# Fused cross-attention and expert layer: gate rows loaded before the zero stores, two tiles gated by VectorE alone, one rounding moved ahead

## The reference, cut to what matters

```python
...
A = jnp.maximum(jnp.abs(masked.sum(axis=0)), 1.0)
O = jnp.einsum('hst,bthe->bshe', A, V).reshape(b, s, dim)
mu = O.mean(axis=-1, keepdims=True)
var = O.var(axis=-1, keepdims=True)
Y = (O - mu) / jnp.sqrt(var + GN_EPS) * gn_gamma + gn_beta
W = jax.nn.relu(x @ wg_w)
return W * Y @ wo_w
...
x = x + attention(layernorm(x), ctx_2048, ctx_2048, ...)
x = x + experts(layernorm(x), ...)
```

## Time and profile before

| quantity | value |
|---|---|
| median of 3 runs | 965.88 us (965.65 to 966.13) |
| span of the profiled execution | 967.2 us |
| PE busy (matmul) | 936.7 us, 97% |
| DVE busy | 518.7 us, 54% |
| POOL busy | 484.5 us, 50% |
| ACT busy | 333.0 us, 34% |

### The profile page before, as it was taken

One profiled execution on the slowest core, in us unless ns is written; L12 is line 12 of the kernel. 1 busy time (PEld: TensorE's weight loads), 2 busy tenths in 40 slices (PEclk: granted clock), 3 DMA queues, 4 the chain that ended last, 5 costly groups with the idle time before them and its releaser, 6 DMA issues.

```text
span 967.2 us, 18994 instructions
## 1 busy us (share of the span) xinstructions
PE 936.7 (97%) x5222; PEld 832.9 (86%) x5223; DVE 518.7 (54%) x1026; ACT 333.0 (34%) x711; POOL 484.5 (50%) x345
## 2 busy tenths in 40 slices
PE   8999998899999989999999999999999999999998
PEld 5767886687889979999999999999999999989886
DVE  5546777888885543333333333333333333349886
ACT  4455554353324222333332333332233333232221
POOL 1116777773176674235535553555555505137760
PEclk9999999999999999999999999999999999999999
DMA  6739994665577667354435555434555422389972
GB/s 210 245 129 392 392 391 156 225 197 152 184 251 260 239 221 249 115 176 161 168 97 179 179 179 175 159 97 170 179 179 179 174 82 77 98 221 266 271 209 85
DMA packets 120646, 187.85 MB, mean 194 GB/s; under 512 B 13600, under 2 KB 71072, under 8 KB 117920
## 3 DMA queue, kind: packets, MB, share of 16 engines
q1 hardware_dynamic: 106704, 107.96, 34.4%
q0 software_dynamic: 13904, 79.44, 24.0%
HBM read 111.85 MB, written 75.50 MB: 194 GB/s over the span
## 4 chain that ended last, share of the span: by engine, by line
PE 78%; DVE 11%; issue 5%; ACT 3%; DMA 2%; POOL 1%; ACTq 0%; DVEq 0%; SPq 0%
PE ps L1050 14%; PE ps L1052 14%; PE ps L1051 14%; PE ps L1102 8%; PE ps L1104 7%; PE ps L1103 7%; PE ps L873 4%; DVE res L1600 2%; PE ps L914 1%; PE ps L923 1%; DVE st L1320 1%; DVE res L1318 1%; DMA gate_d<-gate_out 1%; PE ps L942 1%; PE ps L944 1%
## 5 line engine op out<-in xcount | busy, mean ns | idle before, releaser
L1050 PE MATMUL ps<-whi,xhi 128*128 (+1 forms) x896 | 299.7, 335 | 1.7 <-issue 1.2
L1052 PE MATMUL ps<-whi,xlo 128*128 (+1 forms) x896 | 290.0, 324 | 0.0
L1051 PE MATMUL ps<-wlo,xhi 128*128 (+1 forms) x896 | 289.6, 323 | 0.0
L1050 PEld LDWEIGHTS ps<-whi,xhi 128*128 128x128 f32 x896 | 169.4, 189 | 2.8 <-issue 2.1
L1051 PEld LDWEIGHTS ps<-wlo,xhi 128*128 128x128 f32 x896 | 170.3, 190 | 0.0
L1052 PEld LDWEIGHTS ps<-whi,xlo 128*128 128x128 f32 x896 | 169.2, 189 | 0.0
L783 ACT ACTIVATE sg<-ps 128x352 f32<-128x352 f32 x112 | 52.0, 464 | 299.0 <-PE ps L1052 299.0
L1369 DVE TENSOR_TENSOR hlo<-ps,hhi 128x384 fp32r<-128x384 f32 x112 | 62.3, 556 | 168.3 <-ACT hhi L826 168.2
L1347 DVE TENSOR_TENSOR hx<-ps,sg 128x352 f32<-128x352 f32 x112 | 58.6, 523 | 174.0 <-ACT sg L783 174.0
L527 POOL CAST whi<-raw 128x2816 fp32r<-128x2816 f32 x16 | 40.5, 2534 | 212.2 <-PE ps L1052 212.2
L1102 PE MATMUL ps<-whi,hhi 128*128 (+1 forms) x333 | 132.6, 398 | 4.1 <-DVE hlo L1369 4.1
(11 more groups left out here) (187 smaller groups left out, 1408.9 us busy)
## 6 DMA issues: line engine op xcount, KB each, us to landing
raw<-wexp_in POOLq DMA_DIRECT2D x18, 2176.0 KB, 9.5
xslot_d<-zero SPq DMA_DIRECT2D x10, 2048.0 KB, 21.6
xg<-xslot_d SPq DMA_DIRECT2D x320, 64.0 KB, 2.0
yslot_d<-ysb SPq DMA_DIRECT2D x80, 256.0 KB, 2.1
xg<-xn_d SPq DMA_DIRECT2D x128, 64.0 KB, 3.2
xq<-x_in SPq DMA_DIRECT2D x16, 256.0 KB, 3.5
gate_d<-gate_out SPq DMA_DIRECT2D x16, 256.0 KB, 2.6
yslot_d<-zero SPq DMA_DIRECT2D x2, 2048.0 KB, 18.5
```

The source lines that it names most:

```text
L1050: pe.matmul(ps[:, 2 + m, 0:INTER], xh, wh, start=(k == 0), stop=False)
L1051: pe.matmul(ps[:, 2 + m, 0:INTER], xh, wl, start=False, stop=False)
L1052: mm = pe.matmul(ps[:, 2 + m, 0:INTER], xl, wh, start=False, stop=(k == KT - 1))
```

## The change

Five edits. SP waits for the gate stores and loads gate rows and x rows of tiles 0 and 1 before the zero stores; the pipeline skips them later. `first_gates` on POOL prepares two tiles (four instructions instead of two, over all of head 2's context). On DVE tile 1 gets the same two instructions as tile 0, placed before the second block's statistics; `norm_o(1)`, `affine(1)` and `gate_o(1)` go, and `a_low(0)` moves ahead of `products(last, 2)`. The `wo_remainder` calls of the last two heads move behind the issue of the first expert's load. In the last head ACT rounds strip 0 before it takes the absolute value of strip 1.

```diff
@@ -254,7 +254,7 @@
         scat = sb3("scat", [P, XR, D], F32)
 
         wo_sb = raw[:, 1, 0:KT * D].rearrange("p (k n) -> p k n", k=KT)
-        gate_gamma, gate_beta = head_in[:, 0, 2 * S:3 * S], head_in[:, 0, 3 * S:4 * S]
+        gate_gamma, gate_beta = ([head_in[:, 0, (2 * t + i) * S:(2 * t + i + 1) * S] for t in range(2)] for i in range(2))
         gath = raw[:, :, :].rearrange("p a n -> p (a n)")[:, 0:GR * TOPK * D].rearrange("p (r k n) -> p r k n", r=GR, k=TOPK)
         ps = psum("ps", [P, 8, 512], F32)
 
@@ -354,6 +354,12 @@
             sp.dma_start(gn_sb[:, :, :], gn[None, :, :].to_broadcast([P, 2, D])).then_inc(w3_loaded, 16)
             sp.dma_start(wr_sb[:, :, :], wr.rearrange("(k p) n -> p k n", p=P)).then_inc(w3_loaded, 16)
 
+            for p in range(2):
+                sp.wait_ge(gate_stored[p], 16 * (NT // 2))
+            for t in range(2):
+                sp.dma_start(gin[:, t, :], rows(gate_d, t * ST)).then_inc(gate_loaded[t], 16)
+                sp.dma_start(xin[:, t, :], rows(x, t * ST)).then_inc(x3_loaded[t], 16)
+
             sp.wait_ge(zero_ready, 1)
             for c in range(NR // 8):
                 sp.dma_start(xslot_d[c * 8 * P:(c + 1) * 8 * P, :].rearrange("(p r) n -> p r n", p=P),
@@ -362,18 +368,16 @@
                 sp.dma_start(yslot_d[c * 8 * P:(c + 1) * 8 * P, :].rearrange("(p r) n -> p r n", p=P),
                              zero[:, None, :].to_broadcast([P, 8, D])).then_inc(y_zeroed, 16)
 
-
-            for p in range(2):
-                sp.wait_ge(gate_stored[p], 16 * (NT // 2))
-
             def load_gate(t, r, turn):
-                if type(t) is not int or t >= 2:
-                    sp.wait_ge(gated, t - 1)
+                if type(t) is int and t < 2:
+                    return
+                sp.wait_ge(gated, t - 1)
                 sp.dma_start(gin[:, r % 2, :], rows(gate_d, r * ST + turn)).then_inc(gate_loaded[r % 2], 16)
 
             def load_x3(t, r, turn):
-                if type(t) is not int or t >= 2:
-                    sp.wait_ge(x1_ready, t - 1)
+                if type(t) is int and t < 2:
+                    return
+                sp.wait_ge(x1_ready, t - 1)
                 sp.dma_start(xin[:, r % 2, :], rows(x, r * ST + turn)).then_inc(x3_loaded[r % 2], 16)
 
             def store_xn(t, r, turn):
@@ -486,13 +490,14 @@
                     pool.tensor_tensor(q_lo[:, b, :], q_sb[:, b, :], q_hi[:, b, :].bitcast(F32), ALU.subtract).then_inc(q_rest, 1)
 
             def first_gates():
-                pool.wait_ge(gate_loaded[0], 16)
                 pool.wait_ge(w3_loaded, 48)
                 pool.wait_ge(s_mm, ST * (H - 1))
-                pool.tensor_tensor(gate_gamma, gin[:, 0, :], gn_sb[:, 0, :], ALU.mult).then_inc(gate_affine, 1)
-                pool.tensor_tensor(gate_beta, gin[:, 0, :], gn_sb[:, 1, :], ALU.mult).then_inc(gate_affine, 1)
-                pool.sem_inc(o_gamma, 1)
-                pool.sem_inc(o_beta, 1)
+                for t in range(2):
+                    pool.wait_ge(gate_loaded[t], 16)
+                    pool.tensor_tensor(gate_gamma[t], gin[:, t, :], gn_sb[:, 0, :], ALU.mult).then_inc(gate_affine, 1)
+                    pool.tensor_tensor(gate_beta[t], gin[:, t, :], gn_sb[:, 1, :], ALU.mult).then_inc(gate_affine, 1)
+                pool.sem_inc(o_gamma, 2)
+                pool.sem_inc(o_beta, 2)
 
             def wo_remainder(h):
                 pool.wait_ge(wo_high, h + 1)
@@ -513,9 +518,12 @@
                 if h + 1 < H:
                     q_remainder(h + 1)
                     ctx_remainder(h + 1)
-                wo_remainder(h)
+                if h < H - 2:
+                    wo_remainder(h)
             pool.wait_ge(s_mm, ST * H)
             pool.dma_start(raw[:, 0, :], wexp[0, :, :]).then_inc(raw_loaded[0], 16)
+            for h in range(H - 2, H):
+                wo_remainder(h)
 
             def split(o, p, half, before):
 
@@ -552,7 +560,7 @@
                     pool.wait_ge(first_lo, t + 1)
                     pool.sem_inc(w13_ready, 1)
 
-            for t in range(1, NT):
+            for t in range(2, NT):
                 if t == B:
                     pool.wait_ge(wo_low, KT)
                     pool.wait_ge(o_mm, ST * H)
@@ -690,13 +698,15 @@
                 for j in range(ST):
                     act.wait_ge(s_mm, ST * h + j + 1)
                     n = S - P * j
+                    if j == 1 and h == H - 1:
+                        at_rounded(h, 0)
                     act.activation(at_sb[:, AT_OFF[j]:AT_OFF[j] + n], ps[:, 4 + j % 2, 0:n], ACT.Abs,
                                    scale=const[:, bass.ds(C_KDEC + h * ST + j, 1)]).then_inc(s_abs, 1)
                     if j == 1:
                         act.wait_ge(sum_mm, h + 1)
                         act.wait_ge(o_ready, ST * h)
                         act.activation(v_sum, ps[:, 6, :], ACT.Copy).then_inc(sum_ready, 1)
-                    if j:
+                    if j and (j > 1 or h < H - 1):
                         at_rounded(h, j - 1)
                 at_rounded(h, ST - 1)
                 if h + 1 < H:
@@ -755,8 +765,7 @@
                 act.activation(xT[:, p, :, :], ps[:, p, :], ACT.Copy).then_inc(a_xT, 1)
 
             std_o(0)
-            act.sem_inc(o_normed, 1)
-            norm_o(1)
+            act.sem_inc(o_normed, 2)
             evac_a(0, 0, 0)
             std_o(1)
             norm_o(2)
@@ -1239,15 +1248,15 @@
                     dve.wait_ge(v_ready, ST * h + tt + 1)
                     dve.tensor_tensor(v_lo[:, tt, :], ps[:, V_BANK[tt], :], v_hi[:, tt, :].bitcast(F32), ALU.subtract).then_inc(v_rest, 1)
 
-            def first_centred():
-                dve.wait_ge(gate_affine, 2)
-                dve.wait_ge(o_aggr, 1)
-                dve.scalar_tensor_tensor(gin[:, 0, :], o_sb[:, 0, :], mv3[:, 0, 0:1], gate_gamma, ALU.subtract, ALU.mult).then_inc(o_gated, 1)
-
-            def first_scaled():
+            def centred(t):
+                dve.wait_ge(gate_affine, 2 * t + 2)
+                dve.wait_ge(o_aggr, t + 1)
+                dve.scalar_tensor_tensor(gin[:, t, :], o_sb[:, t, :], mv3[:, t, 0:1], gate_gamma[t], ALU.subtract, ALU.mult).then_inc(o_gated, 1)
+
+            def scaled(t):
                 dve.wait_ge(o_rstd, 1)
-                dve.wait_ge(o_gated, 1)
-                dve.scalar_tensor_tensor(o_sb[:, 0, :], gin[:, 0, :], sd3[:, 1, 0:1], gate_beta, ALU.mult, ALU.add).then_inc(gated, 1)
+                dve.wait_ge(o_gated, t + 1)
+                dve.scalar_tensor_tensor(o_sb[:, t, :], gin[:, t, :], sd3[:, 1, t:t + 1], gate_beta[t], ALU.mult, ALU.add).then_inc(gated, 1)
 
             def a_low(t, r, turn):
                 p, half = r % 2, 2 * turn + r // 2
@@ -1279,15 +1288,16 @@
             last = H - 1
             products(last, 0)
             statistics(last, 0)
-            first_centred()
+            centred(0)
             products(last, 1)
             rstd_o(0)
-            first_scaled()
+            scaled(0)
+            centred(1)
+            scaled(1)
             statistics(last, 1)
+            a_low(0, 0, 0)
             products(last, 2)
             rstd_o(1)
-            gate_o(1, 1, 0)
-            a_low(0, 0, 0)
             products(last, 3)
             a_low(1, 1, 0)
```

## The result

| | before | after |
|---|---|---|
| median of 20 runs | 966.33 us | 969.19 us |
| ratio to before | | 1.0026, 95% interval 1.0017 to 1.0036 |
| span of the profiled execution | 967.2 us | 967.7 us |

The change made the kernel slower by 0.26%, about 2.5 us (interval 1.6 to 3.5). I had forecast 965.7 us, a gain of 0.2 us, with a range of 963.8 to 967.5. Put on the same 965.88 us, the measured ratio gives 968.4.

What follows compares the result with a forecast made beforehand. PE, busy 97% of the span, was taken to bound the kernel; only its waiting stretch could gain. The terms came to -0.22 us at tile 2: profiled 967.2 becomes 967.0, or 965.7 off the 965.88 median, range 963.8 to 967.5.

Steps and rivals of the forecast that it cites:

- The collision of the centring: DVE's centring of tile 0 collides with POOL's first moved remainder of wo and ends at 159.61, 0.26 us later than before.
- the three collisions of the trace before: DVE's centring of tile 0 and gates of tiles 1 and 2, each ending 0.54 to 0.55 us after a POOL instruction.
- POOL's end plus 0.55: Collision rule: a DVE instruction with all operands in SBUF, meeting a POOL instruction, ends 0.55 us after POOL's end.
- The rounding of strip 0: Last head: rounding fits ACT's idle 2.25 us before 151.77, removing POOL's 0.33 us wait; gain 0.33 us.
- The way from tile 0 to the gate of tile 2: Projection stage: statistics to norm 1.76 us, norm to POOL's add 3.68, gate collides, ending at 169.88 against 170.10.
- The late statistics: DVE's statistics of block 1, behind both scalings, start at 162.60 instead of 160.94, 1.66 us later, eating POOL's freed 2.7 us.
- Loads ahead of the zeros, four products: POOL's four gate products start without the 1.54 us DMA wait, ending at 150.2 against 150.5; later zero stores cost 0.
- The pattern of long tiles: Rival: POOL's lag keeps every projection tile long, 4.91 us instead of alternating with 4.09; +3.3 us, 968.9; chance 0.12.
- The escape of tile 2's gate: Rival: DVE's gate of tile 2 gets ahead of POOL's next product, ending at 168.75; gain 1.35, 964.5; chance 0.22.
- Half the worse pattern: Half of the +3.3 us from some 4 short projection tiles becoming long: 967.5, the slow end of the range.
- does not do what it says: Rival: tile 2's gate rows still arrive last, or ACT's new order loses the 0.33 us; 965.9 to 966.4; chance 0.16.
- Were DVE first: Alternative at the centring of tile 0: the remainders slide back and hit its scaling, ending about 161.6; bound +0.7 us.

Runs made afterwards that it cites:

- e1: Changed kernel, but POOL's two remainders of wo wait until tiles 0 and 1 are gated; ratio to before 0.9990 (0.9976 to 1.0003).
- e2: Changed kernel, but the second remainder of wo waits until the first has been written; ratio to before 1.0007 (0.9995 to 1.0018).
- e3: Kernel before with one edit alone: the last two heads' remainders of wo moved behind the expert's load; ratio to before 1.0009 (0.9996 to 1.0022).
- e5: Changed kernel, but each head's remainder of wo stands between POOL's first and second mask; ratio to before 1.0005 (0.9994 to 1.0016).
- e4: Changed kernel with the remainders of wo back in their old places; ratio to before 1.0015 (1.0003 to 1.0027).
- e7: e6 with tile 1 on its old way over ACT, POOL and the gate multiply; ratio to before 0.9989 (0.9974 to 1.0003).
- e8: Kernel before with only the gate and x loads of tiles 0 and 1 ahead of the zero stores; ratio to before 0.9999 (0.9984 to 1.0015).
- e9: e7 plus one more DVE reciprocal, written twice, in front of the projection stage; one run, residual of tile 15 at +92.36 us.
- e10: e6 with the statistics of block 1 ahead of tile 1's two DVE instructions; ratio to before 0.9990 (0.9977 to 1.0003).
- e11: The same kernel as e7, measured again; ratio to before 0.9990 (0.9978 to 1.0001).
- e6: e5 with ACT rounding strip 0 ahead of its wait for strip 1's scores; ratio to before 0.9996 (0.9985 to 1.0008).

## Why the prediction was wrong, point by point

**The collision of the centring: the step that failed.** "It collides and ends at 159.07 + 0.54 = 159.61" takes for granted that DVE gets the port between two POOL instructions. In the three collisions of the trace before, no POOL instruction on SBUF operands was ready behind the one that held DVE: at the gate of tile 1 the next one waited for the one just ended (multiply and add of one tile, spaced 1.42 us), and at the other two POOL's next work was the issue of an expert's load. The two remainders are independent and spaced 1.25 us. DVE was passed over, and the forecast's rule "POOL's end plus 0.55" held with the end of the second: 160.05 + 0.56. That is 1.25 us more than forecast. e1, e2, e3 and e5 show it. The Trainium skill, page SBUF — State Buffer, section "Who interferes with whom", has whoever issues first holding the pair for the whole instruction. The 1.19 us in e4 and 1.78 in e2 agree with that; the 3.01 us of the changed kernel goes beyond one instruction, and the measurement decides.

Why DVE was passed over is not shown, and it does not happen to every instruction. The trace before has a fourth collision, which the prediction left out:

```profile
163.12 0.85 DVE L1230 SCALAR_TENSOR_TENSOR sd<-mv,sd 128x4 f32<-128x4 f32 x1
```

POOL's add of tile 1 ran until 163.95 and its multiply of tile 2, which did not wait for that add, started at 163.91, a spacing of 1.25. This small instruction, 0.16 us alone, still ended at 163.97 and was not held through the second. The same stands in e3, e7, e8, e9, e10 and e11. So the hold through two instructions is seen for the 128x512 centring alone, in two kernels (after and e3).

**The rounding of strip 0: a step that failed.** I put the rounding into ACT's idle 2.25 us before 151.77. In the program it stands behind the wait for strip 1's scores, which is what ended that idle time, as the row said. The wait of 0.33 us on POOL did go, but strip 1's absolute value moved back by half a microsecond: -0.33 forecast, +0.17 measured (+6.91 against +6.74), 0.50 us off. e6 shows it: there the remainder comes at +6.40, the time that the forecast had.

**The way from tile 0 to the gate of tile 2: right.** From the scaling of tile 0 on, the steps came out as worked: statistics to norm 165.48 - 163.72 = 1.76 (1.76 forecast), norm to POOL's add 167.88 + 1.29 - 165.48 = 3.69 (3.68), release of the gate by POOL and not by a DMA, a collision with tile 3's multiply, end at 169.20 + 1.74 = 170.94, 1.77 behind the add (1.84). Only the two instructions of tile 1 took 0.12 us longer, since scaling waits for centring (162.20, 163.05, 163.72).

**What the steps add up to.** Forecast -0.22; the second remainder +1.25; the rounding +0.50; tile 1 +0.12: together +1.65, against +1.58 measured at the residual of tile 0. Behind it came 0.17 us at tile 1's residual, where a 128x4 instruction (177.44, 0.33 us instead of 0.16) met POOL, and 0.36 at tile 5, the open gap. Both were taken as 0 in the forecast, with one collision as the bound. Together 2.12 at tile 15.

**The late statistics: seen, but not weighed.** I wrote that they start 1.66 us later and let that stand as the price of tile 1's new way, balanced by what POOL saved. e10 shows that one line's place decides it: 1.4 us.

**Loads ahead of the zeros, four products: right.** The products ran from 144.39 to 148.14 + 1.28 with no DMA ahead of them, and e8 puts the edit at +0.06 to +0.10.

**The rivals.** The pattern of long tiles did not take over; the short and long tiles alternate in the changed kernel as before. The escape of tile 2's gate did not happen there. It happened in e10 (0.69 us) and nearly in e7 (0.77), which both end about 2 us ahead of before at tile 15; but they hold other repairs too, so they do not price the 1.35 that I gave it. Half the worse pattern, given as 967.5, is 967.3 by its own terms (965.7 + 1.6). The case "does not do what it says" named ACT's new order, and that part came true: the 0.33 us were not gained and 0.17 were lost. Its other part did not: the rows of tile 2 landed at 166.75, before POOL's add began. No case had the hold over two instructions. "Were DVE first" was the only other outcome that I had for that near-tie, and my bound for it, +0.7, was drawn from single collisions.

**What stays open.** The cause of the 0.46 us gap at tile 4, why the hold through two POOL instructions spares the 128x4 ones, and how much faster e7, e10 and e11 are than before: 2 us over the stretch in the traces, about 1 us in the timed runs.

## What to carry to other kernels

Where POOL and DVE both read SBUF, look not only at the POOL instruction that runs but at those queued ready behind it: two independent ones in a row held a two-input DVE instruction of 128x512 through both here, so filler work on POOL belongs where DVE waits anyway, here between two masks. It should not stand ahead of the issue of a load either: here the gate rows of tile 2 landed just behind that load. An instruction is moved ahead only if it is also ahead of the wait that ended the idle time it is meant to fill. When one tile gets a short way, put what the next tiles wait for (here their statistics) ahead of it.

## What the runs showed of the hardware that was not expected

A ready, independent POOL instruction without a gap behind its predecessor kept the waiting centring of DVE out: 3.01 us (after) and 3.00 (e3) with two remainders in a row, 1.78 with a dependency between them (e2), 0.68 with none near (e1, e5). Small operands do not help against one POOL instruction: in e2 a 128x4 instruction of 0.16 us lasted 0.42, and in before one lasted 0.85. But none of 128x4 was held through a second one. A held 128x512 instruction ended 0.54 to 0.56 us behind the POOL instruction that held it, a held 128x4 instruction 0.02.

PE's granted clock fell in the changed kernel. Busy time by stretch, the last columns being clock, DMA share and GB/s:

```profile
170.00:172.00 2.00, 1.01 (x5) 1.01 (x6) 1.97 (x7) 0.00 (x0) 1.86 (x2) 0.74 0.05 7
172.00:174.00 2.00, 2.00 (x6) 1.55 (x6) 1.79 (x8) 0.00 (x0) 1.88 (x3) 0.50 1.00 246
174.00:176.00 2.00, 2.00 (x10) 1.59 (x9) 1.38 (x4) 1.90 (x5) 1.96 (x2) 0.91 0.78 322
```

From a clock of 1.00 it fell to 0.50 (1.2 instead of 2.4 GHz) in 172 to 174. PE had waited 1.97 us for the gate of tile 2 just before, and 2.95 us for tile 0 earlier, at full clock on both sides of that wait. It fell in e2 behind a wait of 1.99 us and in e3 behind one of 2.95, and not in e4, e5 and e6 behind waits of 1.98, so the length of the last wait alone does not tell. It fell on no critical step: the residual of tile 1, at 177.69, was 5.39 us behind that of tile 0, and 5.38 in e7, whose clock stayed at 1.00.
